# Attention over 6404 keys in a fused decoder kernel: the order and tile shape of TensorE's side products, and where in a half they stand

## The reference, cut to what matters

```python
def _L1_xattn_ref(query, key, value, mask, Wq, Wk, Wv, Wo, bo):
    scores = jnp.einsum('bhqd,bhkd->bhqk', Q, K) / jnp.sqrt(jnp.asarray(d_k, Q.dtype))
    scores = jnp.where(mask[:, None] == 0, jnp.asarray(-1000000000.0, scores.dtype), scores)
    attn = jax.nn.softmax(scores, axis=-1)
    Z = jnp.einsum('bhqk,bhkd->bhqd', attn, V)
...
def _L2_xattn_ref(x, context, context_mask, q_w, q_b, kv_w, kv_b, proj_w, proj_b):
    attn = jnp.einsum('bnhd,bshd->bhns', q, k) * scale
    attn = jnp.where(context_mask[:, None, None, :], -jnp.inf, attn)
    attn = jax.nn.softmax(attn, axis=-1)
    out = jnp.einsum('bhns,bshd->bnhd', attn, v).reshape(b, n, c)
```

## Time and profile before

| | us |
|---|---|
| median of three runs | 5968.1 (5966.82 to 5973.21) |
| the profiled execution, its own time | 5964.89 |
| its span in the profile | 5962.8 |
| the masked cross, first to last scores | 1610.3 to 2843.4, that is 1233.1 |
| the plain cross, first to last scores | 3209.7 to 4304.6, that is 1094.9 |

### The profile page before, as it was taken

How to read it: one execution, slowest core, us unless ns; L and a number is a source line. 1 busy time by engine, 2 the same in 40 slices (tenths; PEclk the granted TensorE clock), 3 DMA queues, 4 the chain that set the end, 5 groups by cost and what they waited for, 6 DMA issues and landing times. The chain is left out here.

```text
span 5962.8 us, 93851 instructions
## 1 busy us (share of the span) xinstructions
PE 4230.5 (71%) x35234; PEld 1575.5 (26%) x35234; DVE 3738.2 (63%) x10221; ACT 2479.2 (42%) x3155; POOL 793.5 (13%) x988
## 2 busy tenths in 40 slices
PE   5956999652899999998659999999886721144124
PEld 2333444331222222222431222222244310022012
DVE  5464666554988888884349999999535631146112
ACT  2522666313366666666213777777710100011001
POOL 0000000002000000000020000000000047713772
PEclk9977999776699999999767999999987865567567
DMA  0030000007211121110031111111005000000000
GB/s 13 1 64 10 16 12 9 15 1 278 80 31 31 31 66 30 31 31 12 7 110 35 38 35 31 31 34 31 15 13 165 1 8 13 12 3 6 13 12 8
DMA packets 139821, 206.09 MB, mean 35 GB/s; under 512 B 50877, under 2 KB 103453, under 8 KB 137631
## 3 DMA queue, kind: packets, MB, share of 16 engines
q1 hardware_dynamic: 97758, 181.68, 11.1%
q0 software_dynamic: 20480, 10.53, 1.2%
q10 hardware_dynamic: 21128, 7.88, 0.6%
HBM read 152.65 MB, written 47.35 MB: 34 GB/s over the span
## 5 line engine op out<-in xcount | busy, mean ns | idle before, releaser
L1524 ACT ACTIVATE probs<-ps 128x1024 f32<-128x1024 f32 x1632 | 1580.0, 1022 | 681.4 <-PE ps L1467 679.4
L1550 DVE CUSTOM_DVE_ANT_0 junk<-ps,mask 128x512 bf16<-128x512 f32 (+1 forms) x1664 | 1052.0, 678 | 149.1 <-PE ps L1431 146.8
L1550 DVE CUSTOM_DVE_ANT_0 junk<-ps,nothing 128x512 bf16<-128x512 f32 (+1 forms) x1664 | 1018.2, 677 | 68.4 <-PE ps L1431 67.0
L1431 PE MATMUL ps<-kturned,qturned 49*128 49x512 bf16 (+1 forms) x3328 | 872.4, 399 | 92.4 <-DVE maxima L1550 61.8
L1483 PE MATMUL ps<-probs,vstack 128*18 128x512 f32 x6528 | 878.8, 601 | 0.0
L3218 POOL DMA_INDIRECT line<-table,index x640 | 645.9, 1009 | 878.5 <-DVE index L3591 486.0
L1431 PEld LDWEIGHTS ps<-kturned,qturned 49*128 49x128 bf16 x3328 | 210.8, 93 | 1232.6 <-DVE maxima L1550 739.0
L1467 PE MATMUL ps<-qturned,kturned 52*64 52x512 bf16 x6528 | 521.6, 390 | 8.3 <-ACT probs L1524 7.1
L1454 PE MATMUL ps<-maskT,split 64*128 64x512 bf16 x1632 | 302.4, 383 | 19.9 <-ACT probs L1524 18.5
L1550 DVE DVE_READ_ACCUMULATOR2_ANT maxima<- 128x1 f32 x3328 | 277.4, 83 | 0.0
L2779 PE MATMUL ps<-plane,bands 32*32 32x512 f32 x6720 | 249.6, 608 | 17.5 <-DVE top L2931 17.5
(11 more groups left out here) (720 smaller groups left out, 4817.8 us busy)
## 6 DMA issues: line engine op xcount, KB each, us to landing
vstack<-values_heads SPq DMA_DIRECT2D x128, 229.5 KB, 4.9
raw<-in_mask_BxSxS_if SPq DMA_DIRECT2D x8, 3202.0 KB, 13.5
kturned<-keys_parts SPq DMA_DIRECT2D x384, 54.0 KB
kturned<-keys_parts SPq DMA_DIRECT2D x384, 48.0 KB
table<-lines SPq DMA_DIRECT2D x51, 256.0 KB, 3.1
line<-table,index POOLq DMA_INDIRECT x640
keys_parts<-parts SPq DMA_DIRECT2D x24, 384.0 KB, 2.9
values_heads<-vall SPq DMA_DIRECT2D x2, 3456.0 KB, 12.2
```

Of the source, the lines that this page charges most:

```text
L1431: nc.tensor.matmul(ring(e)[:, 0:hi - lo], qturned[rows, h % 3, m * P:(m + 1) * P], kturned[rows, h % 2, lo:hi], start=True, stop=True).the ...
L1524: nc.scalar.activation(probs[:, u % slots].rearrange("p b n -> p (b n)"), k.ps[:, bank:bank + 2, :].rearrange("p b n -> p (b n)"), ACT.Exp ...
L1550: nc.vector.tensor_tensor_reduce(junk[:, at % RING, 0:hi - lo], ring(e)[:, 0:hi - lo], lost, 1.0, -3.0e38, ALU.subtract, ALU.max, maxima[: ...
```

## The change

It has four parts, all inside `programme` and TensorE's block of `cross`:

1. The parts of a half are spread over all its 51 units instead of the first 49.
2. In the masked cross the two units of a round take turns: masks, scores, masks, scores, instead of masks of both and then scores of both.
3. A piece that stands behind the scores is made by two products of 64 columns of weights, one for the upper and one for the lower 64 partitions of its bank, instead of by one of 128. The sum of the two is the same piece; one semaphore tells of both.
4. In the plain cross the pieces behind the weighing are made in this way too; in the masked cross they stay one product. Two markers in the list (`behind_weighing`, `behind_scores`) switch between the two ways; other engines pass them over. The pieces ahead of the first round stay whole.

By the list, 770 of 1664 pieces of the masked cross and 1544 of 1664 of the plain one are made in two products, so TensorE has 2314 products and as many loads of weights more than before.

```diff
@@ programme()
-        cut = [-(-len(parts) * min(t, KT - 2) // (KT - 2)) for t in range(KT + 1)]
+        cut = [-(-len(parts) * t // KT) for t in range(KT + 1)]
...
-        out += [("scores", 2 * g)] + spread[2 * g] + late.pop(g, []) + spread[2 * g + 1]
+        out += [("scores", 2 * g)] + spread[2 * g] + [("behind_weighing",)] + late.pop(g, []) + spread[2 * g + 1] + [("behind_scores",)]
@@ cross(), the tensor block
-            def piece(e):
+            def piece(e, parts):
...
-                nc.tensor.matmul(ring(e)[:, 0:hi - lo], qturned[rows, h % 3, m * P:(m + 1) * P], kturned[rows, h % 2, lo:hi],
-                                 start=True, stop=True).then_inc(ring_filled, 1)
+                for part in parts:
+                    last = nc.tensor.matmul(ring(e)[part, 0:hi - lo], qturned[rows, h % 3, m * P + part.start:m * P + part.stop],
+                                            kturned[rows, h % 2, lo:hi], start=True, stop=True, skip_group_check=True)
+                last.then_inc(ring_filled, 1)
...
+            whole, quarters = [slice(0, P)], [slice(0, 64), slice(64, P)]
+            parts = whole
             for e in steps:
                 if e[0] == "piece":
-                    piece(e)
+                    piece(e, parts)
+                elif e[0] == "behind_weighing":
+                    parts = whole if maskT is not None else quarters
+                elif e[0] == "behind_scores":
+                    parts = quarters
                 elif e[0] == "scores":
-                    if maskT is not None:
-                        masks(e[1])
-                        masks(e[1] + 1)
-                    score(e[1])
-                    score(e[1] + 1)
+                    for u in (e[1], e[1] + 1):
+                        if maskT is not None:
+                            masks(u)
+                        score(u)
```

## The result

| | before | with the change |
|---|---|---|
| median | 5967.5 us (4 runs, 5965.4 to 5973.2) | 5912.4 us (4 runs, 5901.2 to 5917.1) |
| the profiled execution, its own time | 5964.9 | 5917.1 |
| its span | 5962.8 | 5915.2 |
| masked cross, first to last scores | 1233.1 | 1187.8 |
| plain cross | 1094.9 | 1083.8 |

A forecast was written before the change was run, and what follows sets the result against it. Masked cross bound by a ScalarE-TensorE loop, plain cross by VectorE's pieces and a small loop; masked -53.5 (-34 - 2 - 12.5 - 5) and plain -21 make -74.5 from 5964.9: 5890.4, median 5893 us, range 5874 to 5929.

The forecast's parts named there:

- The loop of the masked cross: Masked cross: ScalarE and TensorE wait for each other, setting 2.78 us a round with or without pieces; turns cut it.
- The new masked round: Masked cross, rounds with two pairs: TensorE's own sequence sets 2.73 us instead of 2.78, -0.05 a round.
- scores to masks 0.32 (as to pieces): Masked round in turns: the step from first scores to second masks takes 0.32 us, as to pieces of the masks' shape.
- Two halves of the masked cross: Masked cross: spread and shorter rounds together take 4.9 us off every two halves, seven times that -34.
- The stretches of low clock: Masked cross: three stretches at half clock, 1.6 us each, should not come once the waits are filled: -5 us.
- In the loop of rows 8 both changes of shape stay, so I take nothing: Plain cross, loop of VectorE and TensorE (1.86 us against 1.83): quarters change nothing, bounds 0.03 less or 0.02 more a round.
- The spread: Plain cross: VectorE's idle time at a half's end goes, 1.5 us per half over 14 halves, -21 us.
- the turns with their quarters: Masked cross: -0.05 us a round with two pairs, -0.52 a round without pieces (half 15: -12.5), three pairs 3.80 to 3.93.
- the quarters save nothing: Rival, masked cross: scores to pieces takes 0.32 instead of 0.24 in some 350 rounds, +28, 5921 us; chance 0.13.
- The wait is not what holds the masked cross: Rival, masked cross: the loop only hides a TensorE limit, +0.08 a round, 5956 us, about no change; chance 0.05.
- VectorE is late no more: Rival, plain cross: quarters end VectorE's lateness of 0.03 us a round, -11, 5882 us; chance 0.06.
- the slower one: Rival, both crosses: a piece's two quarters don't run together, a pair takes 0.44 us more, about 6200 us; chance 0.06.

The follow-up runs named there:

- r5: The kernel before with only the new spread: 5913.6 us (4 runs), ratio 0.9910; masked cross 1202.6 us, plain cross 1074.3.
- r7: The kernel before with only the quarters, old order and old spread: 5965.4 us in one run; masked cross 1221.9 us, plain cross 1104.8.
- r8: The changed kernel without the turns (spread and quarters kept): 5914.1 us in one run; masked rounds 2.776 us, half 15 69.7 us.
- r6: The kernel before with only masks and scores in turn, pieces whole, old spread: 5992.5 us (5 runs), ratio 1.0039; masked rounds 2.848 us.
- r2: The changed kernel with all pieces of the plain cross whole: 5903.2 us (4 runs), ratio 0.9873; plain rounds 2.483 us.
- r11: The changed kernel with quarters in the plain cross only behind the weighing, those behind the scores whole: 5919.2 us in one run; plain rounds 2.503 us.
- r12: The changed kernel with all pieces of the masked cross whole, turns and spread kept: 5944.3 us in one run; masked rounds 2.847 us.
- r3: The changed kernel with quarters in the plain cross only behind the scores, those behind the weighing whole: 5912.5 us in one run; plain rounds 2.498 us.
- r9: The changed kernel with plain-cross pieces whole and no turns in the masked round behind one with three pairs: 5887.7 us (4 runs), ratio 0.9859.
- r10: The changed kernel with the plain cross's weighing cut in two around the piece that waits for VectorE: 6182.3 us; plain rounds 3.24 us.
- r4: The kernel of r2 with each plain-cross piece made by two products over half of the keys: 5900.0 us in one run; plain rounds 2.489 us.

## Why the prediction was right, and where it was off

The sign and the range (5874 to 5929) held, and so did the mechanism in the masked cross and that of the spread. The step on the quarters in the plain cross did not. The gain was 55 us by the medians instead of 75. Point by point:

- *The loop of the masked cross* held: 2.775 us whatever the rounds contain (r5, r7, r8), and it is gone with the turns (half 15: 2.308).
- *The new masked round* was 2.743, forecast 2.73. The term that was off is "scores to masks 0.32 (as to pieces)": it is 0.333. Scores that follow a change of shape directly, as a unit alone does in turns, last 0.400 us a product instead of 0.376 (those of a second group), and the next change of shape comes 0.02 later. The row was there: the plain cross before has such a lone unit in its half 15, with 0.34 us to the next shape.

```profile
4295.21 0.41 PE L1467 MATMUL ps<-qturned,kturned 52*64 52x512 bf16 x4 [0.21 <-ACT probs L1524]
...
4295.55 1.05 PE L1483 MATMUL ps<-probs,vstack 128*18 128x512 f32 x8
```

A round fell by 0.032, not 0.05 (0.013 from the new round, 0.005 because I took 2.775 as 2.78): over 33 rounds in seven pairs of halves this is 4 us of the 8 by which the forecast was short, and in half 15 it is 1.5 more.
- *Two halves of the masked cross*, -4.9 forecast, gave -4.3 us in the middle (low clock left out) and -2.6 at the first; half 14 gave 0.8 instead of 2.
- *The stretches of low clock* went from the masked cross, -5 as forecast (they fell at halves 2, 10 and 12, each 1.6 us longer than the others). The reason that I gave, that they should not come once the waits are filled, isn't shown: r6 and r7 keep the old spread and have none there either, and r2, r11 and r12 have one each, where half 15 begins. That the plain cross would get two or three instead I had not forecast: 1.1 us each, 3 us in the profile. It has none in the kernel before and in r6, whose plain crosses are the same program, and two to five in all the others. The spread alone is enough (r5 has three, with all pieces whole), and so are the quarters alone (r7 has three, with the old spread). Why is open.
- *"In the loop of rows 8 both changes of shape stay, so I take nothing"* is the step that failed. Both stay, but each is dearer by the quarters: 0.015 for a lone quarter piece ahead of the weighing, 0.020 for the pair behind it, which ends later (r3, r11). My bound was 0.02 a round. Two halves take 138.2 us with it and 136.9 without (r2), 1.3 us each, so 9 us over seven pairs.
- *The spread* in the plain cross: -21 forecast, -20.6 with pieces whole (r5). That it agrees so well is in part luck: two halves fell by 3.3 us (140.2 to 136.9) where I had 3.0, which is 23 us over seven pairs, and three stretches of low clock took 3 back. The same holds for the 1074 us of r2. So the plain cross's 11 us are 23 from the spread less 9 for the quarters and 3 for the clock.
- *The parts against each other.* The spread's share of the forecast was near: 27 and 5 us in the masked cross and 21 in the plain one, 53 in all, against 51 (r5). The rest, 21 us from the turns with their quarters, was 5: the quarters on top of the spread give 5 us in the masked cross and a loss of 9 in the plain one (r5 to r8), and the turns on top of both give 10, by half 15 alone (r8 to the changed kernel). I had priced the turns at -0.05 a round in some 260 rounds, and did not set against it that without them, but with quarters, the rounds with three pairs would be 3.69. The parts depend on each other: alone, the turns cost 16 us in the masked cross (r6), or 21 with the low clock of before left out.

Of the rivals, "the quarters save nothing" falls: the step from scores to pieces is 0.24 (rows above), and whole pieces take 0.34 (r6). "The wait is not what holds the masked cross" falls with half 15 (2.775 to 2.308), and "VectorE is late no more" with the plain round of 2.52. So does the slower one: the two products of a piece start together (four in 0.39 us). The Trainium skill's rule that a load overlaps running products only where the row group differs ("TensorE: Matmul & The Clock Gate", Part 3, The mechanism) does not hold here if taken by itself: quarters that use the rows of the scores before them start 0.24 after those, while the scores are drawn 0.40 long. (The same section of the Trainium skill also lets a load go ahead into a background weight buffer, which fits these rows.) The Trainium skill's rule that a change of tiling mode drains TensorE ("TensorEngine Tiling (Array Packing)", Key Properties) holds in so far as each change costs 0.08 to 0.10 us; that the array is empty in between, no run here shows. r6, with six changes a round instead of four, is the case where it decides the sign.

## What to carry to other kernels

Look for the loop first: a round that takes the same time with and without a part of its work, as here 2.775 us, is not set by that work, and here it was set by two engines that wait for each other. What fills that wait (here the quarters without the turns) is worth nothing in those rounds. When the loop is cut, look how near the next bound is, here 0.03 us, and each change of tile shape that the cut costs has to be paid from that. Run the parts apart: here one line carried 51 of the 56 us of the crosses, and taking the others out where they lose gave another 20 us there (r9). And compare stretches that the clock left alone: three short stretches of low clock were enough to make a term that was off look exact.

## What the runs showed of the hardware

- A change of tile shape costs 0.08 to 0.10 us on TensorE. From the last start of one group to the first of the next it is 0.230 us from scores to quarters or scores, in the same shape. With a change it is 0.308 behind a second group (scores to whole pieces before; quarters to weighing after) and 0.333 behind a group that stands alone (scores to masks after; scores to whole pieces in r6).
- The first group of 64 by 64 tiles behind a change is drawn 0.400 us long, the next 0.376; products of 128 columns are 0.386 and 0.378. The ends are the profile's model, but the starts agree: the next change comes 0.025 us later behind the longer one. In the plain cross's loop through VectorE this was 0.015 and 0.020 us a time (r3, r11).
- Four f32 products with 18 columns, side by side in 32-column tiles, take 0.99 us to the next group, and two take 0.97 (r10).
- 1544 more products with their loads of weights cost the plain cross 2 us (r4 against r2, each with two stretches of low clock).
